# Attention kernel: half of the token groups projected between score steps, packed maxima, layer norm on GpSimd

## The reference

```python
c_kv = x @ W_dkv.T                               # 128 latents
q = (x @ W_dq.T @ W_uq.T).reshape(B, T, 16, 16)
k_eff = (W_dq.T @ W_uq.T @ W_uk).reshape(16, 16, 128)
v_eff = transpose((W_uv.T @ W_o.T).reshape(128, 16, 16), (1, 0, 2))
attn = einsum('bhql,bkl->bhqk', einsum('bqhd,hdl->bhql', q, k_eff), c_kv) / sqrt(16)
attn = softmax(where(causal, attn, -inf))
y = einsum('bhql,hld->bqhd', einsum('bhqk,bkl->bhql', attn, c_kv), v_eff)
# layer norm: (x - mean(x)) / sqrt(var(x) + 1e-5)
```

## Time and profile before

| | before |
|---|---|
| median of 3 runs | 1482.82 us (1481.82 to 1488.69) |
| profiled execution, its own time | 1484.99 us |
| its span | 1482.8 us |
| TensorE busy (matmuls) | 1224.4 us, 83% |
| VectorE busy | 986.0 us, 66% |
| ScalarE busy | 591.5 us, 40% |
| GpSimd busy | 345.6 us, 23% |
| mean granted TensorE clock | 0.92 |

### The profile page before, as it was taken

One profiled execution on the slowest core, in us unless ns is written; L12 is line 12 of the kernel. 1 busy time (PEld: TensorE's weight loads), 2 busy tenths in 40 slices (PEclk: granted clock), 3 DMA queues, 4 the chain that ended last, 5 costly groups with the idle time before them and its releaser, 6 DMA issues. The chain is left out here.

```text
span 1482.8 us, 32889 instructions
## 1 busy us (share of the span) xinstructions
PE 1224.4 (83%) x13850; PEld 770.9 (52%) x13850; DVE 986.0 (66%) x2188; ACT 591.5 (40%) x999; POOL 345.6 (23%) x495
## 2 busy tenths in 40 slices
PE   5638899999999999998999726558798868689993
PEld 3314444444444444436888613335565656578883
DVE  4527788888888888835754656676868372375546
ACT  3415565556565656575322222112232212142222
POOL 2313200000000000001211256535563312221114
PEclk9869999999999999998999958878898988889996
DMA  5692333344433334200000000001111101000003
GB/s 177 115 155 95 137 44 44 45 57 59 59 45 44 45 45 61 28 2 1 1 1 1 1 29 10 22 21 37 31 33 26 37 20 18 2 0 1 0 1 113
DMA packets 77795, 61.69 MB, mean 42 GB/s; under 512 B 41168, under 2 KB 63824, under 8 KB 77520
## 3 DMA queue, kind: packets, MB, share of 16 engines
q1 hardware_dynamic: 76496, 57.18, 21.9%
q10 hardware_dynamic: 1152, 2.41, 0.5%
HBM read 38.20 MB, written 20.97 MB: 40 GB/s over the span
## 5 line engine op out<-in xcount | busy, mean ns | idle before, releaser
L651 DVE TENSOR_REDUCE maxima<-psum 128x1 f32<-128x512 f32 (+3 forms) x768 | 395.2, 553 | 65.5 <-PE psum L426 47.6
L619 ACT ACTIVATE weights<-psum 128x1024 f32<-128x1024 f32 (+3 forms) x384 | 296.2, 813 | 198.5 <-PE psum L454 142.0
L423 PE MATMUL psum<-k_stack,q_stack 96*128 96x512 bf16 (+3 forms) x768 | 236.1, 329 | 33.1 <-DVE maxima L651 33.0
L451 PE MATMUL psum<-q_stack,k_stack 99*128 99x512 bf16 (+3 forms) x768 | 202.2, 326 | 1.2 <-ACT weights L619 1.2
L423 PEld LDWEIGHTS psum<-k_stack,q_stack 96*128 96x128 bf16 x768 | 74.6, 97 | 196.2 <-DVE maxima L651 121.9
L468 PE MATMUL psum<-weights,v_rows 128*17 128x512 f32 (+3 forms) x1536 | 161.1, 491 | 0.0
L392 POOL TENSOR_TENSOR residual<-residual,att_o 128x256 f32<-128x256 f32 x32 | 23.2, 724 | 486.6 <-DVE att_o L686 486.6
L848 PE MATMUL psum<-f_xT,f_weights_hi 128*128 128x512 f32 x384 | 123.9, 404 | 0.0
L913 ACT ACTIVATE f_gates<-psum,ffn_biases 128x512 f32<-128x512 f32 x72 | 49.5, 687 | 155.9 <-PE psum L854 155.9
L426 PE MATMUL psum<-mask_scores,identity 128*128 128x128 bf16 x512 | 110.6, 221 | 0.0
L1284 PE MATMUL psum<-d_w_qkb,d_hT 128*128 128x260 f32 x128 | 48.4, 514 | 66.2 <-DVE d_attnT_k_kb_v L1454 55.6
(11 more groups left out here) (160 smaller groups left out, 2253.1 us busy)
## 6 DMA issues: line engine op xcount, KB each, us to landing
qk_parts<-a_parts SPq DMA_DIRECT2D x32, 384.0 KB, 2.6
q_stack<-qk_parts SPq DMA_DIRECT2D x96, 128.0 KB, 7.4
k_stack<-qk_parts SPq DMA_DIRECT2D x96, 128.0 KB, 8.1
residual<-in_x SPq DMA_DIRECT2D x8, 512.0 KB, 7.6
out_x<-residual SPq DMA_DIRECT2D x8, 512.0 KB, 3.8
ffn_weights<-in_ffn_w ACTq DMA_DIRECT2D x1, 2048.0 KB, 8.8
systems<-d_a_rows SPq DMA_DIRECT2D x32, 64.0 KB, 1.8
d_systems<-systems SPq DMA_DIRECT2D x4, 512.0 KB, 3.3
```

Source lines behind the costliest of these rows:

```text
L423: m = e.matmul(bank[bk][:, 0:width], self.qst[st][0:SCORE_ROWS, h, qb * P:(qb + 1) * P], self.kst[st][0:SCORE_ROWS, h, k0:k0 + width], sta ...
L451: m = e.matmul(out[:, 0:width], self.kst[st][0:SCORE_ROWS + MAX_ROWS, h, kb * P:(kb + 1) * P], self.qst[st][0:SCORE_ROWS + MAX_ROWS, h, q0 ...
L619: e.activation(self.weights[n % 2][:, 2 * pair:2 * pair + 2, 0:width], self.st_pair[pair][:, :, 0:width], ACT.Exp, scale=HS ** -0.5).then_ ...
L651: e.tensor_reduce(self.maxima[n][:, h, qb, k0 // BANK:k0 // BANK + 1], next_max_bank()[:, 0:width], AXIS_X, ALU.max, negate=True).then_inc ...
```

## The change

What the changed kernel does:

- One list says in which order all engines work. `order` writes it: `prologue` (groups 0 and 1, then groups 2 and 3 interleaved with 46 maxima) and `during`, one list of items for each step. Groups 4 to 7 are projected in the steps: ten items each (two turns, two latents, four q/k products, two value products), one in every second step from steps 4, 26, 48 and 70 on. In a step, half of the items stand between the two score pairs, the rest behind the second, then come the values.
- A maxima item fills a bank: heads whose tiles fit in one bank of 512 columns share it and are reduced together, 38 items per unit for 48. One mask matmul covers all heads of an item and comes first. The negated maxima's transpose stands two items behind the last maximum of its unit.
- In the prologue seven banks rotate over all items; in the steps banks 4 to 6 rotate over maxima, projections and outputs.
- Unit 0's stack is loaded in two halves, behind groups 0 and 1; units 1 and 2 are loaded behind group 1.
- `xT` is one buffer of its own, `lat` two; `rest` has two buffers for four. The weights used only at the start lie where the exps' buffer will be.
- `Norm`: all statistics ahead of all aggregates on DVE; GpSimd computes the negated mean too and normalises. The three memsets of ones in `k_stack` are DVE's first work.

```diff
 class Norm: (vector)
             e.bn_stats(k.stats[:, t, :], k.xr[:, t, :]).then_inc(*s["stats"].did(i, t))
+        for t in tiles:
             for w in unmet(s["stats"](i, t)):
                 e.wait_ge(*w)
             e.bn_aggr(k.moments[:, t, :], k.stats[:, t, :]).then_inc(*s["moments"].did(i, t))
-        for j, t in enumerate(tiles):
-            for w in unmet(s["rstd"](i), s["turned"](i - len(self.slots), KT - 1) if i >= len(self.slots) else None):
-                e.wait_ge(*w)
-            e.tensor_scalar(self.slot(i)[:, j, :], k.xr[:, t, :], k.moments[:, t, 0:1], k.rstd[:, t:t + 1],
-                            ALU.subtract, ALU.mult).then_inc(*s["normed"].did(i, j))
 (gpsimd)
         e.tensor_scalar(k.rstd[:, g], k.moments[:, g, 1], EPS, None, ALU.add).then_inc(*s["eps"].did(i))
+        e.tensor_scalar(k.negmean[:, g], k.moments[:, g, 0], -1.0, None, ALU.mult).then_inc(*s["negmean"].did(i))
...
+        for j, t in enumerate(tiles):
+            for w in unmet(s["rstd"](i), s["negmean"](i), s["turned"](i - len(self.slots), KT - 1) if i >= len(self.slots) else None):
+                e.wait_ge(*w)
+            e.tensor_scalar(self.slot(i)[:, j, :], k.xr[:, t, :], k.negmean[:, t:t + 1], k.rstd[:, t:t + 1], ALU.add, ALU.mult
+                            ).then_inc(*s["normed"].did(i, j))
 class Attention:
+    LEAD = 8
+    PROLOGUE_BANKS, RING = (0, 1, 2, 3, 4, 5, 6), (4, 5, 6)
...
-        self.per_unit = [(h, qb, c * BANK, min(BANK, (qb + 1) * P - c * BANK)) for qb in range(QB) for h in range(HPU)
-                         for c in range(((qb + 1) * P + BANK - 1) // BANK)]
+        self.pairs = []
+        for qb in range(QB):
+            for c in range(((qb + 1) * P + BANK - 1) // BANK):
+                width = min(BANK, (qb + 1) * P - c * BANK)
+                n = min(HPU, BANK // width)
+                self.pairs += [(qb, c, width, range(h, h + n)) for h in range(0, HPU, n)]
...
+    def order(self):
+
+        per = len(self.pairs)
+        maxima = []
+        for u in range(len(self.units)):
+            maxima += [("max", u, w) for w in range(per)]
+        late = {}
+        for u in range(len(self.units)):
+            late[min((u + 1) * per + 2, len(maxima)) - 1] = ("negmax", u)
+
+        def project(g):
+            return ([("turn", g, kt) for kt in range(KT)] + [("lat", g, n) for n in range(2)] +
+                    [("qk", g, *p) for p in self.PROJECTED] + [("v", g, j) for j in range(0, TPG, 2)])
...
+        self.taken, lead = 0, per + self.LEAD
+        more = project(2) + [("norm", 4)] + project(3)
+        self.prologue = [("norm", 0), ("norm", 1), ("const", 0), ("const", 1), ("const", 2)] + project(0) + [("norm", 2)]
+        self.prologue += project(1) + [("norm", 3)]
+        for i in range(lead):
+            self.prologue += take(i + 1) + more[i * len(more) // lead:(i + 1) * len(more) // lead]
+        self.during = [[] for _ in range(len(self.steps) + 3)]
+        for g in range(4, GROUPS):
+            first = 4 + (g - 4) * 22
+            for i, item in enumerate(project(g)):
+                self.during[first + 2 * i].append(item)
+            if g > 4:
+                self.during[first - 8].append(("norm", g))
+        for n, (u, kb, qc) in enumerate(self.steps):
+            self.during[n] += take(lead + -(-per * (n + 1) // len(self.unit_steps)))
+            if kb == (qc + 1) * TPG - 1:
+                self.during[n + 2].append(("out", u, qc))
+        self.bank, self.released, held, at = {}, {}, {}, 0
+        for ring, items in [(self.PROLOGUE_BANKS, self.prologue)] + [(self.RING, items) for items in self.during]:
+            for item in items:
+                if item[0] != "norm":
+                    b = ring[at % len(ring)]
+                    at += 1
+                    self.bank[item] = b
+                    self.released[item] = held.get(b)
+                    held[b] = self.release(item)
...
 (sync)
+        for item in self.prologue:
+            send(item)
+            if item == ("qk", 0, *self.PROJECTED[-1]):
+                load(0, (0,))
+            if item == ("qk", 1, *self.PROJECTED[-1]):
+                load(0, (1,))
+                for u in range(1, STACKS):
+                    load(u, (0, 1))
+        for n, items in enumerate(self.during):
+            if n and n % len(self.unit_steps) == 0 and n // len(self.unit_steps) - 1 + STACKS < len(self.units):
+                load(n // len(self.unit_steps) - 1 + STACKS, (0, 1))
+            for item in items:
+                send(item)
...
 (tensor)
+                if diagonal:
+                    e.matmul(out[:, 0:len(heads) * width].rearrange("p (h x) -> p h x", h=len(heads))[:, :, width - P:width],
+                             k.ident16[:, :], k.mask16[:, :].rearrange("p (o x) -> p o x", o=1).to_broadcast([P, len(heads), P]),
+                             start=True, stop=False, skip_group_check=True)
+                for i, h in enumerate(heads):
+                    m = e.matmul(out[:, i * width:(i + 1) * width], self.qst[st][0:self.ROWS, h, qb * P:(qb + 1) * P],
+                                 self.kst[st][0:self.ROWS, h, k0:k0 + width], start=not diagonal and i == 0, stop=True,
+                                 skip_group_check=True)
...
+        for n, items in enumerate(self.during):
+            half = len(items) // 2
+            if n < len(self.steps):
+                scores(n, 0)
+            for item in items[:half]:
+                make(item)
+            if n < len(self.steps):
+                scores(n, 1)
+            for item in items[half:]:
+                make(item)
+            if 0 < n <= len(self.steps):
+                values(n - 1)
...
 (scalar: exp of the first pair, then the items' copies, then exp of the second pair)
+        for n, items in enumerate(self.during):
+            if n < len(self.steps):
+                exps(n, 0)
+            for item in items:
+                copy_out(item)
+            if n < len(self.steps):
+                exps(n, 1)
+            if 0 < n <= len(self.steps):
+                turn_out(n - 1)
```

More of the change, by code:

```diff
@@ L297, in __init__, with take @@
         self.unit_steps = [(kb, qc) for qc in range(QC) for kb in range((qc + 1) * TPG)]
         self.steps = [(u, kb, qc) for u in range(len(self.units)) for kb, qc in self.unit_steps]
-        self.n_max = len(self.units) * len(self.per_unit)
-        self.lead = len(self.per_unit) + MAX_LEAD
+        self.order()
+    def order(self):
[9 more added lines that the diff above has]
+                    [("qk", g, *p) for p in self.PROJECTED] + [("v", g, j) for j in range(0, TPG, 2)])
+        def take(n):
+            out = []
+            for i in range(self.taken, min(n, len(maxima))):
+                out += [maxima[i]] + ([late[i]] if i in late else [])
+            self.taken = max(self.taken, min(n, len(maxima)))
+            return out
+        self.taken, lead = 0, per + self.LEAD
[24 more added lines that the diff above has]
+                    held[b] = self.release(item)
+            if items is self.prologue:
+                self.prologue_end = dict(held)
@@ L302, in part, with release @@
+    def release(self, item):
+        s, kind, a = self.s, item[0], item[1:]
+        if kind == "const":
+            return s[("wukq_out", "keff_out", "veff_out")[a[0]]]()
+        if kind == "qk":
+            return s["rest"](self.part(*a))
+        return s[{"turn": "xT_out", "lat": "lat_out", "v": "v_out", "max": "max_red", "negmax": "max_rest", "out": "att_o"}[kind]](*a)
     def part(self, g, which, mt):
@@ L333, in max_tiles @@
[L333 to L344 removed]
+            cols = slice(halves[0] * BANK, (halves[-1] + 1) * BANK)
@@ L366, in sync @@
-        max_tiles(max(self.lead - at, 0))
-        for n, (u, kb, qc) in enumerate(self.steps):
-            max_tiles(3)
-            if n and n % len(self.unit_steps) == 0 and u - 1 + STACKS < len(self.units):
-                load(u - 1 + STACKS)
-            max_tiles(1)
+        for item in self.prologue:
[6 more added lines that the diff above has]
+                    load(u, (0, 1))
@@ L437, in turn, with stacked @@
-        def turn(g):
-            for kt in range(KT):
-                self.ln.tensor(e, unmet, g, kt, bank[kt], s["xT_out"](g - 1, kt) if g else None)
-        def scores(u, n, kb, qc, pair):
-            st = u % STACKS
-            q0 = max(qc * BANK, kb * P)
-            width = (qc + 1) * BANK - q0
-            diagonal = kb * P >= qc * BANK
-            for w in unmet(s[f"stack_in{st}"](u, PRODUCTS - 1, 1), s[f"max_in{st}"](u, MAX_ROWS - 1), s["k_ones"](st),
-                           *([s["exp"](n - 1, pair)] if n else [free.get(2 * pair), free.get(2 * pair + 1)])):
+        def stacked(u, half):
+            return s[f"stack_in{u % STACKS}"](u, half if u == 0 else 1, self.PRODUCTS - 1, 1)
@@ L448, in scores @@
+        def scores(n, pair):
+            u, kb, qc = self.steps[n]
+            st = u % STACKS
```

(34 more changed lines are left out.)

559 lines of the change are left out of this document (240 added, 319 removed).

## The result

The changed kernel takes 1489.89 us (median of 20 runs, 1485.27 to 1493.72) against 1484.74 (median of 20, 1479.75 to 1488.69): a ratio of 1.0036, 95% interval 1.0024 to 1.0048. It is slower by some 5 us; 1466 was forecast, with 1440 to 1500 as the range. The profiled execution of the new kernel is its fastest one (1485.27 us, span 1483.5), 0.7 us over the span of before, so the two profiles are compared stage by stage and not by their sum. One run of the kernel before with the output moved took 2411.93 us, far from the three others (1504.67 to 1510.13), and is left out of its median.

A forecast was written before the change was run, and what follows sets the result against it. TensorE was taken to bound the steps and feed-forward stages, latency the prologue. Terms -59 + 61 - 16.7 - 2 = -16.7 us, from the median 1482.82, gave 1466 us; range 1440 to 1500.

The forecast's parts named there:

- The bound: Whole kernel: TensorE full in attention steps (31 us of work a unit) and feed-forward; latency bounds the stretch before the steps.
- Part 1: Prologue: four groups and 46 maxima instead of eight and 64; step 0 near 111 us, -59 us (-68 to -52).
- Part 2: Attention steps: projections of groups 4 to 7 add 40 us of TensorE work plus stalls, +61 us (+46 to +80).
- the rival of the copy chain: Steps: in-order ScalarE and VectorE copies hold the exps at every projected item; 1502 us, chance 0.18.
- the prediction's own sign: The prediction is wrong if the prologue gains less than 50 us or the steps lose more than 60.
- Part 3: Steps: new order and packing of the maxima, -16.7 us, from -20 to -3.
- the closing of the hole: Negated maxima's transpose: TensorE's 1.24 us wait for VectorE goes in fifteen units, -18.6 us.
- The rows come late: Start of a unit: maxima sent later stall TensorE 0.3 us in the eight units without projections, +2.4 us.
- Ten fewer instructions: Packed maxima in each unit: ten fewer TensorE instructions, estimated at 10 ns each, -1.5 us over all units.
- The sign given for this part: Units 8 to 15: 31.2 us expected; at 32.3 the maxima forecast is wrong and first score pairs wait for the rows' DMA.
- Part 4: Feed-forward stages, norm on GpSimd: -1 us at each start, -2 together (-4 to +3); later TensorE hides everything.
- The rows of maxima come late: Rival, in the steps: one more us of landing in each unit, +15, 1481 us; chance 0.20 shared with other near-equal cases.

The follow-up runs named there:

- LEAD = 12: The changed kernel with the output item last in its step and four more maxima items made ahead of the steps (12 for 8): 1472.77 us, ratio 0.991.
- 1431.52: The kernel before with the transpose two tiles later, norm on GpSimd, loads of units 0 to 2 behind groups 1, 3, 5: 1431.52 us, ratio 0.9634.

## Why the prediction was wrong, point by point

**The bound.** Right: TensorE's stream bounds the steps and the feed-forward stages, latency the prologue. The kernel with the later transpose shows the unit at 31.02 us, the forecast's sum being 31.

**Part 1, -59 us: measured -57.4.** The first score matmul stands at 112.63 us, forecast at 111; ACT's wait for a store ends at 102.08, forecast at 98 or 99. These are the two rows of the changed kernel:

```profile
102.08 0.60 ACT L646 ACTIVATE a_parts<-psum 128x512 bf16<-128x512 f32 x1 [3.61 <-DMA qk_parts<-a_parts]
...
112.63 0.38 PE L575 MATMUL psum<-q_stack,k_stack 99*128 99x512 bf16 x1 [0.34 <-DVE negmax L706]
```

The wait is 3.61 us and not 10, since ACT came there at 98.5 and not at 88: the loads of units 1 and 2 were issued from 67.42 us on (forecast 61), and the order reached group 3 some 10 us later. The store landed only 3 to 4 us late, and what stands behind the wait took 10.6 us for the 12.4 forecast. That the sum came within 2 us is in part luck: errors offset each other. The working also took GpSimd's normalising as a small cost; in the kernel before, together with the new order of the statistics, it brings step 0 forward by 10.8 us, with DVE's 11.8 us of waits for the factor gone.

By the Trainium skill (DMA: Bandwidth & Descriptors, on queues, rings and completion order), the descriptors of one issuing engine's ring are consumed in ring order on each DMA engine. The traces agree: stores issued behind 36 loads land after 25.4 us in the median, between packs of twelve after 7.0.

**Part 2, +61 us: measured +61.1** as the difference of two kernels that differ in nothing else. The working had 40 us of stream and 21 of stalls; about 20 us of holes at the bank ring were counted in units 0 to 7 of the kernel with `LEAD = 12`, and 9.4 us went when the order changed. The seven units with projections took 40.3 us in the mean in the changed kernel, between 36.2 and 44.7 each, where the forecast had 39 and the rival of the copy chain 42; they differ since ten items over twenty steps fall unevenly on units of twelve. With the output last they take 39.5 in the mean, and the forecast stands. By the prediction's own sign the steps were not to lose more than 60 us; they lost 62.8, and it is part 3 that took them over it.

**Part 3, -16.7 us: the step that failed.** Its parts: the closing of the hole (-18.6) is shown alone at -18.3. The rows come late by 5.2 us in holes, 5.6 by the experiment, against +2.4: the mechanism was right, the size was off by a factor of two, inside the stated bounds. The forecast spread it evenly, 0.3 us in eight units; the waits are 0.25 to 0.69 in five units and 1.97 in the last. Ten fewer instructions a unit were to give 1.5 us; the packed unit of 31.11 us beside the unpacked one of 31.02 shows no such gain. What is missing altogether is the output: the wait of its transposes, for ACT's copy and in half of the cases for their bank, stands in no term, and was put at nothing without a reason. "By the counts" I followed the maxima through the new lists and never asked in which place the output lands in its list; the kernel before has it behind the second pair, and I carried this place over. It costs 16.3 us in holes; undoing it gives 14.1 by the stages and 11 by the medians, and putting it into the kernel before costs 22. With -18.6 + 5.4 + 16.3 the part is +3.1 for -16.7, and the sum -59 + 61 + 3.1 - 2 is +3 for a measured +5. The sign given for this part came true: the unit did not reach 31.2 us. The wait for the rows that was named with it is there too, but is the smaller share.

**Part 4, -2 us: measured -1.4 and -0.4, no more than the scatter.** Over the twelve profiles the first feed-forward stage takes 171.4 to 173.2 us with the norm on GpSimd (eight) and 172.8 to 173.5 with it on DVE (four), 1.0 apart in the mean; the second shows no difference (172.7 to 173.9, 173.1 to 173.3). In the feed-forward stretch DVE has 40.95 us for 63.91 and GpSimd 38.89 for 20.62, and TensorE 100.00 of 100.00 as in the earlier trace rows. The second turn's wait is 1.49 us for 3.71:

```profile
691.28 1.12 PE L248 MATMUL psum<-identity,normed 128*128 128x128 f32 x4 [1.49 <-POOL normed L240]
```

By the Trainium skill (SBUF — State Buffer, on the shared port pair) GpSimd and some DVE instructions lock each other out. The traces agree: in the kernel before ten normalisations take 2.49 us, each beside a multiplication of the gates of 2.40 us (L793) on GpSimd; the forecast had counted twelve. But 23 us less of DVE's time in 100 changed neither stage by 2 us: the full PE decided, as the row said.

**The rivals and chances.** Each had a price worked out, but none was of the kind that happened. "The rows of maxima come late" holds 3 of the 19 us missing. A trace of before shows only where the output stood; that the new order puts it elsewhere stood in the diff, in one `append`. The chance for slower was 0.18 for a copy chain; a misplaced item in an order written anew belonged there as well. The range's working doesn't come out either: the four parts' own bounds add up to -29 and +45 us, or to -18 and +25 if they vary independently, and not to -40 and +25.

**Open.** A kernel with all of the good parts (all groups ahead, output last, spread loads, packed maxima) wasn't run, so whether the packing adds to 1431.52 is not shown; in the full steps it gave nothing (31.11 us a unit for 31.02).

## What to carry to other kernels

Where one list sets the order of all engines, write down for each item on the bound engine which engine makes its input, when that engine gets to it, and what stands between; an output moved up by a few places cost 0.5 to 0.7 us each time, twice a unit, and that took back what closing the transpose's hole had given. Moving work of a bound engine between stages need not gain anything: four groups cost 61.6 us ahead and 61.1 inside here. Such a balance hangs on the order at both ends (51.7 inside with another order, and a wait of 16.4 us ahead), so look for the waits at both before moving. The plain wait in the profile, 25 us behind 36 loads on one queue, was the largest gain to be had, and it took a change of three lines.

## What the runs showed of the hardware

Two things I had not expected. Spreading the loads may have done more than shorten the queue. With 36 loads queued the DMA engines were full and moved 147 GB/s between 80 and 100 us; with packs of twelve the same stretch reads

```profile
80.00:100.00 20.00, 17.42 (x72) 8.82 (x71) 14.61 (x34) 10.97 (x20) 11.66 (x14) 1.00 0.70 168
```

168 GB/s at a share of 0.70, though with another mix of loads and stores in it, so that the rates of the two can't be told apart here. And code that no experiment touched, the delta stage, took between 438.1 and 445.0 us in twelve profiled executions, more than the whole effect of the change: a difference of a few us has to be read from the stage that was changed, or from medians.
